# A decoder layer on one core: the feed-forward's token channels read by indirect DMA instead of one-hot matmuls

## The reference, cut to what matters

```python
def _L0_ffn_ref(x, gate_w, W, atoms, expert_atom_weights, importance, mask_idx):
    xt = x.reshape(-1, H)                       # 896 tokens x 256 channels
    logits = jnp.clip(xt @ gate_w.T, -50.0, 50.0)
    top_w, top_idx = jax.lax.top_k(logits, TOP_K)      # 2 of 8 experts
    rw = jax.nn.softmax(top_w, axis=-1)
    deltas = jax.nn.softmax(expert_atom_weights, axis=-1) @ atoms
    weighted = deltas * jax.nn.sigmoid(importance)     # 8 x 2048
    rows = mask_idx // H
    cols = mask_idx % H
    vals = jnp.einsum('tk,tks->ts', rw, weighted[top_idx])
    xg = xt[:, cols]                            # the gather: 2048 channels of each token
    contrib = jax.ops.segment_sum((xg * vals).T, rows, num_segments=H)
    return (xt @ W.T + contrib.T).reshape(B, S, H)
```

## Time and profile before

| | |
|---|---|
| median of 3 runs | 983.55 us (983.32 to 983.77) |
| the profiled execution, own time | 986.56 us |
| its span, first to last instruction | 984.8 us |
| mean granted TensorE clock | 0.959 |
| PE busy, share of the span | 914.5 us, 93% |
| DVE / ACT / POOL busy | 556.1 / 564.8 / 74.5 us |
| cross-attention's block ends, feed-forward's first matmul | 889.7 us |

### The profile page before, as it was taken

How to read it: one execution, slowest core, us unless ns; L and a number is a source line. 1 busy time by engine, 2 the same in 40 slices (tenths; PEclk the granted TensorE clock), 3 DMA queues, 4 the chain that set the end, 5 groups by cost and what they waited for, 6 DMA issues and landing times. The chain is left out here.

```text
span 984.8 us, 19351 instructions
## 1 busy us (share of the span) xinstructions
PE 914.5 (93%) x7803; PEld 783.0 (80%) x7803; DVE 556.1 (56%) x1054; ACT 564.8 (57%) x976; POOL 74.5 (8%) x83
## 2 busy tenths in 40 slices
PE   5945989999999999999999999999999999989995
PEld 3534579898989898989898988888888888877773
DVE  2695465656564656565655565656565556553424
ACT  2513166767575657565766666666666665653442
POOL 0021000000000000000000000000000000063453
PEclk9965699999999999999999999999999999989998
DMA  6009557575757565666666666666766676400001
GB/s 177 7 23 267 150 132 171 128 172 133 161 135 159 145 150 146 147 155 141 159 150 158 139 160 151 158 139 159 154 159 138 159 152 140 93 15 1 2 1 37
DMA packets 67816, 126.13 MB, mean 128 GB/s; under 512 B 23568, under 2 KB 52408, under 8 KB 67512
## 3 DMA queue, kind: packets, MB, share of 16 engines
q1 hardware_dynamic: 66384, 124.66, 53.1%
q10 hardware_dynamic: 1344, 0.23, 0.2%
HBM read 46.30 MB, written 4.65 MB: 52 GB/s over the span
## 5 line engine op out<-in xcount | busy, mean ns | idle before, releaser
L1248 ACT ACTIVATE probsT<-ps_T 125x448 f32<-125x448 f32 x384 | 195.2, 544 | 181.8 <-PE ps_T L1122 181.8
L1349 DVE CUSTOM_DVE_ANT_0 scores<-ps_scores,mask_sb 112x1500 f32<-112x1500 f32 x128 | 219.7, 1716 | 79.5 <-PE ps_scores L1111 75.1
L1122 PEld LDWEIGHTS ps_T<-ident,scores 112*125 112x125 f32 x1536 | 200.6, 189 | 17.6 <-ACT probsT L1248 3.1
L1122 PE MATMUL ps_T<-ident,scores 112*125 112x112 f32 x1536 | 207.9, 271 | 2.1 <-ACT probsT L1248 2.0
L1238 ACT ACTIVATE scores<-scores,shift 112x1500 f32<-112x1500 f32 x128 | 197.1, 1540 | 0.9 <-DVE shift L1349 0.9
L1091 PE MATMUL ps_proj<-room,wkvT 128*128 128x500 f32 x576 | 158.5, 411 | 6.2 <-DVE room L1332 3.3
L1136 PE MATMUL ps_out<-probsT,v_sb 125*32 125x112 f32 x3072 | 161.3, 262 | 0.0
L1099 PE MATMUL ps_proj<-wkvT,room 128*125 128x256 f32 x1152 | 159.7, 289 | 0.5 <-DVE v_sb L1327 0.4
L1136 PEld LDWEIGHTS ps_out<-probsT,v_sb 125*32 125x32 f32 x3072 | 145.8, 111 | 15.6 <-issue 10.6
L1099 PEld LDWEIGHTS ps_proj<-wkvT,room 128*125 128x125 f32 x1152 | 146.5, 189 | 10.3 <-issue 4.3
L1336 DVE SCALAR_TENSOR_TENSOR room<-ps_proj,xbk,room 128x500 fp32r<-128x500 f32 x96 | 70.7, 737 | 125.0 <-ACT room L1233 124.9
(11 more groups left out here) (252 smaller groups left out, 616.8 us busy)
## 6 DMA issues: line engine op xcount, KB each, us to landing
k_stack<-room SPq DMA_DIRECT2D x384, 187.5 KB, 4.0
ctx_rows<-in_ctx SPq DMA_DIRECT2D x48, 500.0 KB
mask_sb<-in_mask_BxSxS_ff SPq DMA_DIRECT2D x32, 328.1 KB
q_stack<-q_hi SPq DMA_DIRECT2D x32, 112.0 KB, 5.3
q_hi<-k_stack SPq DMA_DIRECT2D x4, 448.0 KB, 3.8
q_lo<-k_stack SPq DMA_DIRECT2D x4, 448.0 KB, 4.0
q_stack<-q_lo SPq DMA_DIRECT2D x16, 112.0 KB, 5.3
ctx_rows<-in_L_ffn_mask_idx SPq DMA_DIRECT2D x1, 1024.0 KB, 5.7
```

The lines of the kernel that those rows point to most:

```text
L1122: last = nc.tensor.transpose(ps_T[0:LT, (TB * t + k) % 2, j * PN:(j + 1) * PN], scores[:, t % 2, (k * TC + j) * LT:(k * TC + j + 1) * LT], ...
L1248: nc.scalar.activation(probsT[:, t % 2, k * TC:(k + 1) * TC], ps_T[0:LT, (TB * t + k) % 2, 0:TC * PN].rearrange("p (j n) -> p j n", j=TC), ...
L1349: nc.vector.tensor_tensor_reduce(out=split(scores[:, t % 2], NC), in0=ps_scores[0:PN, :, 0:LC], in1=split(mask_sb[:, a], NC), scale=-1.0, ...
```

## The change

The transposed tokens are also copied unrounded to `x2T` in SBUF (one more ScalarE copy for each `T` unit) and stored to DRAM as a table of 256 rows (channels) by 448 tokens, one table per half (`store_transposed`, SP). POOL then issues 16 indirect DMAs per half (`gather_on_gpsimd`), each fetching 128 rows of 1792 bytes by `col_i`, into `xg`, 16 tiles of 128 x 448. The first half's are issued while batch 15 runs; after them POOL waits for the last scores and makes `pick_r`, whose place is now behind the products in the key stacks. The second half's are issued once the first half's product of the same step has been taken, after POOL's last `prod_lo`. The gather matmuls, `pick_c`, `idx_row` (1 MB load) and the copies out of PSUM are gone. In the first half POOL makes `prod_lo` of the even steps and VectorE of the odd ones; in the second VectorE makes all. The steps are no longer one loop over both halves: the first half is scattered to its end, followed by `dense(1)`, unit `C` and `back(0)`, and only then the second half starts.

```diff
-        "pick_c": split(take("room", KT * NS), KT),
-        "pick_r": split(take("room", NST * D), NST),
+        "xg": split(take("room", NST * HALF, dt=F32), NST),
+        "pick_r": split(keep["k_stack"][:].rearrange("p k l -> p (k l)")[:, 2 * BUFS * HALF:2 * BUFS * HALF + NST * D], NST),
+        "x2T": split(take("context", 2 * KT * HALF), 2 * KT),
...
+def store_transposed(sp, io, keep, h):
+
+    sp.wait_ge(keep["x2T_full"], KT * (h + 1))
+    sp.dma_start(io["x2T"][h].rearrange("(m p) t -> p m t", p=P), expert_room(keep)["x2T"][:, KT * h:KT * (h + 1)]).then_inc(keep["x2T_stored"][h], 16)
+
+
+def gather_on_gpsimd(nc, pool, io, keep, h, j):
+
+    e = expert_room(keep)
+    nc.gpsimd.indirect_dma_start(e["xg"][:, j], None, io["x2T"][h], bass.IndirectOffsetOnAxis(ap=e["col_i"][:, j:j + 1], axis=0)
+                                 ).then_inc(keep["xg_in"][j // 2], 16)
...
     if u[0] == "T":
+        nc.scalar.activation(expert_room(keep)["x2T"][:, KT * h + u[1]], bank[:, 0:HALF], ACT.Copy).then_inc(keep["x2T_full"], 1)
...
                 batch(B - 2, B // 2 - 1, 0, AT_R, True, False)
+                store_transposed(sp, io, keep, 0)
                 stack_shares(sp, keep, 0, unit_out, units_before(last, 1) + AT_LAST[("C", 0, 0)] + 1 + 2)
...
+                pool.wait_ge(keep["col_ready"], 1)
+                pool.wait_ge(unit_in_psum, units_before(last, 1))
                 for p in range(NP):
                     pool.wait_ge(k_in[p], 16 * STACK * B)
+                pool.wait_ge(keep["x2T_stored"][0], 16)
+                for j in range(NST):
+                    gather_on_gpsimd(nc, pool, io, keep, 0, j)
+
+                pool.wait_ge(scores_in_psum, B * NP)
                 rows_on_gpsimd(nc, pool, keep)
...
                     if t == 0:
-                        columns_on_vector(nc, dve, keep, 0)
                         rows_on_vector(nc, dve, keep)
-                    if t == 1:
-                        for p in range(NP):
-                            dve.wait_ge(k_in[p], 16 * STACK * B)
-                    if t in (1, 3):
-                        columns_on_vector(nc, dve, keep, {1: 1, 3: 2}[t])
...
-HIDDEN_AT = {0: 0, 1: 1, 3: 2, 4: 3, 6: 4, 7: 5, 9: 6, 10: 7, 13: 8}
-GAP_AT = 11
-DENSE_AT = {0: -1, 1: 15}
+HIDDEN_AT = {0: [0], 2: [1], 5: [2], 6: [3], 10: [4], 11: [5], 13: [6], 14: [7]}
+BEHIND = 8
+CENTRE_AT, POW_AT = 8, 8
+GAP_AT = NST - 1
...
+                store_transposed(sp, io, keep, 1)
                 stack_shares(sp, keep, 1, late_out, len(HIDDEN))
...
+                for n in range(NST):
+                    if on_pool(n):
+                        pool.wait_ge(prod_hi_ready, n + 1)
+                        if n >= BUFS:
+                            pool.wait_ge(contributed, n - BUFS + 1)
+                        nc.gpsimd.tensor_tensor(prod_lo[:, n % BUFS], prod[:, n % BUFS], prod_hi[:, n % BUFS].bitcast(F32), ALU.subtract).then_inc(lo_pool, 1)
+                    if n == POW_AT:
                         result_on_gpsimd(nc, pool, keep, NT - 1)
+                pool.wait_ge(keep["x2T_stored"][1], 16)
+                for j in range(NST):
+                    pool.wait_ge(prod_ready, j + 1)
+                    gather_on_gpsimd(nc, pool, io, keep, 1, j)
...
-                pe.wait_ge(keep["column_steps"], 1 + KT)
-                gather(0)
-                gather(1)
+                values(0)
+                values(1)
                 dense(0)
+                pe.wait_ge(keep["row_steps"], 2 + NST)
+                for h in range(2):
+                    for j in range(NST):
+                        n = h * NST + j
+                        if n >= 2:
+                            values(n)
+                        if j >= LAG:
+                            scatter(n - LAG)
+                        if h == 0:
+                            for k in HIDDEN_AT.get(n, []):
+                                hidden(k)
+                    for n in range((h + 1) * NST - LAG, (h + 1) * NST):
+                        scatter(n)
+                    if h == 0:
+                        dense(1)
+                        hidden(BEHIND)
+                    back(h)
...
+                for h in range(2):
+                    for j in range(NST):
+                        n = h * NST + j
+                        dve.wait_ge(keep["xg_in"][j // 2], 32 * (h + 1))
+                        dve.wait_ge(vals_in_psum, n + 1)
+                        if n >= BUFS:
+                            wait_lo(dve, n - BUFS)
+                        nc.vector.tensor_tensor(prod[:, n % BUFS], ps[:, 2 + n % 2, 0:HALF], xg[:, j], ALU.mult).then_inc(prod_ready, 1)
+                        if j > 0:
+                            low(n - 1)
+                        if h == 0:
+                            for k in HIDDEN_AT.get(n, []):
+                                late(k)
+                        if n == CENTRE_AT:
+                            centre(nc, dve, keep, NT - 1)
+                    low(n)
+                    if h == 0:
                         shares_on_vector(nc, dve, keep, 1)
+                        late(BEHIND)
                         normalise(0)
                 normalise(1)
```

More of the change, by code:

```diff
@@ L616, in expert_room @@
         "channel_row": take("context", D),
-        "channel": take("context", KT),
+        "col_i": take("context", NST, dt=I32),
         "idx_col": take("context", NST, dt=I32),
@@ L687, in rows_on_gpsimd @@
     pool.wait_ge(steps, 2)
-    pool.wait_ge(keep["channels"], 3)
+    pool.wait_ge(keep["channels"], 2)
     for j in range(NST):
         nc.gpsimd.tensor_scalar(e["pick_r"][:, j], e["channel_row"], e["row_f"][:, j:j + 1], None, ALU.is_equal).then_inc(steps, 1)
[L693 to L701, removed]
 def late_unit_on_tensor(nc, keep, u, h, bank):
@@ L1486, in kept @@
         "q_stored": ctx.enter_context(nc.semaphore("q_stored")),
+        "stored": ctx.enter_context(nc.semaphore("stored")),
         "outT": sb("outT", [P, 2, 2 * PN]),
@@ L1545, in kept_later @@
         "idx_col_in": sem("idx_col_in"),
-        "idx_row_in": sem("idx_row_in"),
         "row_steps": sem("row_steps"),
-        "column_steps": sem("column_steps"),
+        "col_ready": sem("col_ready"),
+        "x2T_full": sem("x2T_full"),
+        "x2T_stored": [sem(f"x2T_stored{h}") for h in range(2)],
+        "xg_in": [sem(f"xg_in{j}") for j in range(NST // 2)],
         "x2T_hi_ready": sem("x2T_hi_ready"),
@@ L1605, in feed_forward_phase, with on_pool, lo_before, wait_lo @@
         y_ready = sem("y_ready")
-        stored = sem("stored")
+        stored = keep["stored"]
         def tiles(h):
             return range(h * HT, (h + 1) * HT)
+        def on_pool(n):
+            return n < NST and n % 2 == 0
+        def lo_before(n, pool):
+            return sum(on_pool(k) == pool for k in range(n))
+        def wait_lo(engine, n):
+            if on_pool(n):
+                engine.wait_ge(lo_pool, lo_before(n, True) + 1)
+            else:
+                engine.wait_ge(lo_dve, lo_before(n, False) + 1)
         with nc.Block() as block:
@@ L1646, in dense @@
                             nc.tensor.matmul(ps[:, 4 + 2 * h + m, 0:HALF], w, x, start=n == 0, stop=False)
-                def gather(n):
-                    h, j = UNIT[n]
-                    if n >= 2:
-                        pe.wait_ge(xg_copied, n - 1)
-                    if (h, j) == (1, 0):
-                        pe.wait_ge(late_out, 1 + HIDDEN.index(("T", 1, 0)))
-                    mm = [(pick_c[:, m, j * P:(j + 1) * P], part[:, m]) for m in range(KT) for part in x2T_parts(keep, h)]
-                    for k, (w, x) in enumerate(mm):
-                        last = nc.tensor.matmul(ps[:, n % 2, 0:HALF], w, x, start=k == 0, stop=k == len(mm) - 1)
-                    last.then_inc(xg_in_psum, 1)
                 def values(n):
@@ new lines, in low @@
+                def low(n):
+                    if not on_pool(n):
+                        dve.wait_ge(prod_hi_ready, n + 1)
+                        if n >= BUFS:
+                            dve.wait_ge(contributed, n - BUFS + 1)
+                        nc.vector.tensor_tensor(prod_lo[:, n % BUFS], prod[:, n % BUFS], prod_hi[:, n % BUFS].bitcast(F32), ALU.subtract).then_inc(lo_dve, 1)
+                for h in range(2):
+                    for j in range(NST):
+                        n = h * NST + j
+                        dve.wait_ge(keep["xg_in"][j // 2], 32 * (h + 1))
+                        dve.wait_ge(vals_in_psum, n + 1)
+                        if n >= BUFS:
+                            wait_lo(dve, n - BUFS)
+                        nc.vector.tensor_tensor(prod[:, n % BUFS], ps[:, 2 + n % 2, 0:HALF], xg[:, j], ALU.mult).then_inc(prod_ready, 1)
+                        if j > 0:
+                            low(n - 1)
+                        if h == 0:
+                            for k in HIDDEN_AT.get(n, []):
+                                late(k)
```

(5 more changed lines are left out.)

93 lines of the change are left out of this document (21 added, 72 removed).

## The result

The changed kernel takes 995.25 us (median of four, 993.81 to 999.14), beside 983.43 us for the kernel before (median of four): a ratio of 1.0128, with a 95% interval of 1.0098 to 1.0157. It is slower by 11.8 us, where I had forecast 979.8, faster by 3.8, and put 0.40 on slower. So the direction was wrong. The time lies inside the range of 970 to 996, whose upper end I had drawn for another reason, dear indirect DMAs. The profiled execution has a span of 993.3 us, 12.3 more than the 981.0 of my sum.

The account below looks back on a forecast made before the run. TensorE was taken to bound the feed-forward, with POOL's queue delaying its start: 900.3 start + 64.4 halves + 12.0 tail + 4.3 clock = 981.0 us span, 3.8 under 984.8, so 979.8 us; 8 in 10 between 970 and 996.

Parts of the forecast that it names:

- item 6: Tail and clock: tail 12.0 us as before; lower clock charged at 2.8 us for the start, 1.5 for the turn.
- item 5: Second half: 16 scatters and 12 values, 20.7 us, 1.39 per step, ending at +64.4; VectorE just keeps up.
- Item 1: Last batch: without the VectorE wait some 6 us less, TensorE through near 883, hidden behind POOL.
- Item 2: Feed-forward's start: POOL's table wait, 16 indirect DMAs and 16 masks put it at 900.3 us, 10.6 later.
- g: Price of one indirect DMA on POOL, taken as 1.1 us, with ends 0.34 and 2.1.
- Items 3 and 4: First half and turn: last scatter at +33.1, unit C at +36.1, then 7.6 us to the next scatter at +43.7.
- A: POOL beside the last batch: dear indirect DMAs, deciding from g = 1.34; 991.0 us at 1.8, 1001 at 2.1; chance 0.32.
- D: Last batch: table lands, or POOL reaches it, only when batch 15 is nearly over; 988.3 us; chance 0.04.
- B: POOL's indirect DMAs cheap as SP's 0.34 us: time 969.5 us, at 0.7 973.4; chance 0.14.
- C: VectorE's moved `prod_lo`s held behind POOL, 0.95 us each for four: 983.6 us, no visible difference; chance 0.10.

Follow-up runs that it names:

- the turn filled: Changed kernel plus 26 unused matmuls at the turn between the halves: 981.74 us (ratio 0.9971); in a later set 1011.53 us.
- the split gathers: Changed kernel, row masks on VectorE, eight of the first half's sixteen indirect DMAs moved into the feed-forward: 965.71 us with the turn filled, 979.37 us not filled.
- unit C first: The split gathers with the turn filled, but unit C ahead of `dense(1)` and 22 unused matmuls: 964.17 us (ratio 0.9797).
- the run of 999.40: The kernel with unit C first run again unaltered, in another set: 999.40 us (ratio 1.0158).

## Why the prediction was wrong

**The step that failed** is in item 6, "With 14 wide matmuls at half speed I charge 2.8, and 1.5 for the turn". The charge for the start holds; the one for the turn was a small fixed sum, as if the clock came back by itself, and the 1.39 us a step of item 5 rests on that. What the runs show in its place is a state: the clock falls in the turn's pause and five matmuls a step leave it down until the half is over. From the first scatter of the second half (945.82) to its end (981.27) it took 35.45 us where I had 20.7 and the 1.5: 13.3 us too little. That is more than the whole miss of 12.3; the first scatter of the second half was 1.0 early. With the turn filled the total came to 981.74 against my 979.8. The rows for it were there in part: the batch with the wait had a mean clock of 0.77, and I used it for the price of a slow matmul and not for asking what makes the clock come back.

**Item 1** holds: the 3.67 us wait is gone and the last batch ends at 881.4 (I had 883), and none of it shows in the total.

**Item 2** gave 900.3 and the start was 900.5, but by terms that cancel. The indirect DMAs took 20.0 us, not 18.8 (1.25 each where I took 1.1; the first 0.28 longer, not 1.2). The masks took 14.4, not 16.7: the first had no surcharge any more, which is 1.2 of it, and the others had 0.90 each from start to start, where the 16.7 held longer ones. The block's end took 1.7 us and not 0.3. The mechanism is shown by the split gathers: 17.5 us earlier with the shorter queue and the masks on VectorE. That the sum came within 0.2 us is luck. I had put both ends of g far apart (0.34 and 2.1), and the nearest row, 1.15, was the right one to choose.

**Items 3 and 4** hold: the half's last scatter came at +35.1 from the start (33.1, and 2.8 for the clock), unit C at +38.0 (38.9), the second half's first scatter at +45.3 (46.5). I had the turn's length right (7.6 us, measured 7.9) and charged the fall of the clock in it with 1.5 us, without asking what brings the clock back.

**Item 5** is right at the clock that it supposed: 1.40 us per step with the turn filled, against 1.39. Its fear that VectorE just keeps up did not come true, for at either clock VectorE waits.

**The rivals.** I had called the 0.40 on slower A and D, but these are 0.32 and 0.04, and part of A lies within 0.2%: the rivals as written add up to at most 0.36. *A* decides from g = 1.34; g was 1.25, so it was not this that made the kernel slower. That most of the chance on slower stood on it is luck. *B* and *D* did not happen; the indirect DMAs began at 864.4, in the last batch. *C* has a trace in the changed kernel: VectorE's residual addition (L802), beside POOL's subtraction, took 1.04 us. It costs little there. Its stronger form, POOL's DMA behind VectorE's masks, appeared only when an experiment put the two side by side. No rival had the clock for its mechanism, though the row with 0.77 asked for one.

## What to carry to other kernels

Work taken out of a matmul-bound loop is worth its time only if TensorE keeps its clock: price the loop at both levels, look for the last pause ahead of it, and ask whether what is left of the loop can bring the clock back. A dozen useless matmuls beside a pause were worth 8 us here, as long as the pause stayed short. When work is moved to an idle engine, write out that engine's whole queue up to the next barrier, for its length becomes the start of the next stage. And run a design with indirect DMAs in several sets, on more than one chip, before its gain is believed.

## What was not expected of the hardware

- The same matmuls, with TensorE busy 98% of the time by the profile, ran at 1.2 GHz for 37 us in one kernel and at 2.4 GHz in another. Only what stood before them differed. The Trainium skill (TensorE: Matmul & The Clock Gate, Part 1) says that activity releases the throttle; here the throttle stayed at a busy share of 98%, so the profile's share does not tell whether it will be released.
- Five profiles show the same pause of 1.76 or 1.77 us for POOL's pow in the first half (the kernels with the gathers split, filled or not, and with unit C first). In three of them the clock fell behind it, in two it did not, one of these the fastest run of its kernel (972.01 us). Where it fell, it came back within the first half: with unit C first at 916.2, in the fourth of six matmuls of unit `L` in a row; with the gathers split and the turn filled only in a row of 16 scatter matmuls, 916.3 to 921.9. With a pause of 0.62 us it stayed up in both profiles.
- An indirect DMA of 128 rows of 1792 bytes costs POOL 1.25 us in the changed kernel's first row of 16, first to last without change (0.94 to 0.95 busy, 1.23 the first), and lands 3.2 to 4.3 us after its issue.
- The stops: in three sets of six, ScalarE and VectorE stood still for up to 9.5 us at a time (VectorE in the last batch of the run of 999.40), mostly while POOL issued indirect DMAs, in all seven profiles of kernels with them. TensorE had idle times without a releaser beside them (7.38 us in the one above). No profile of the other three sets has a wait called remote in the last batch or the feed-forward, and the kernel before kept its time in all six (983.4 to 985.6 us). One chip was in a set of either kind, so it isn't the chip alone. The Trainium skill (SBUF — State Buffer, Who interferes with whom) has it that ScalarE never waits for another engine's ports; what ScalarE waits for here is not shown by these runs, and the cause stays open.
